# A hybrid of convolution attention, additive attention and a mixture of experts on one core: another ordering rule for TensorE's work in the planner

## What is computed

```python
# layer 0, x is group-normed, (4, 128, 4096)
e1, e2, asm = prelu(w1 @ x), prelu(w2 @ x), prelu(wa @ x)
score = softmax(einsum('nci,ncj->nij', e1, e2), axis=2)
x = x + einsum('nij,ncj->nci', score, asm)
# layer 1, t is the tokens (4, 4096, 128), n = layer norm of t
f, g = n @ W1[:128], n @ W1[128:]
th = tanh(f[:, :, None, :] + g[:, None, :, :] + b1)        # 4096 x 4096 x 16, lower triangle
e = exp(einsum('bija,a->bij', th, w2) + b2) * tril
t = t + einsum('bij,bjh->bih', e / e.sum(-1), n)
# experts: gate, softmax over positions, 8 best positions of each expert, two layers, added back
```

## Time and profile before

| | |
|---|---|
| median of three runs | 6187.79 us |
| the profiled execution, time and span | 6179.02 us, 6177.2 us |
| TensorE busy | 5525.7 us (89%) |
| ScalarE busy | 4999.0 us (81%) |
| VectorE busy, GpSimd busy | 2151.3 us, 2015.0 us |
| mean granted clock of TensorE | 0.947 of full |

### The profile page before, as it was taken

One profiled execution on the slowest core, in us unless ns is written; L12 is line 12 of the kernel. 1 busy time (PEld: TensorE's weight loads), 2 busy tenths in 40 slices (PEclk: granted clock), 3 DMA queues, 4 the chain that ended last, 5 costly groups with the idle time before them and its releaser, 6 DMA issues.

```text
span 6177.2 us, 73459 instructions
## 1 busy us (share of the span) xinstructions
PE 5525.7 (89%) x29478; PEld 1611.1 (26%) x29588; DVE 2151.3 (35%) x3588; ACT 4999.0 (81%) x4234; POOL 2015.0 (33%) x1644
## 2 busy tenths in 40 slices
PE   6999988999999978999999988999999986766756
PEld 2233222222223222222223232222223231111122
DVE  8521137641212257641212257641212161000232
ACT  0127889999888889999888879999888889999930
POOL 0265431124454511124454511125455521111100
PEclk8999999999999989999999979999999998889966
DMA  0000000000000010000000010000000010000037
GB/s 24 1 14 7 8 28 4 1 1 4 11 8 14 8 44 4 1 1 4 11 8 14 9 30 18 1 1 4 8 11 14 8 33 6 1 1 1 11 139 235
DMA packets 31282, 115.99 MB, mean 19 GB/s; under 512 B 4512, under 2 KB 5088, under 8 KB 25632
## 3 DMA queue, kind: packets, MB, share of 16 engines
q1 hardware_dynamic: 30944, 111.30, 5.4%
HBM read 81.60 MB, written 29.49 MB: 18 GB/s over the span
## 4 chain that ended last, share of the span: by engine, by line
PE 69%; issue 13%; ACT 10%; DVE 6%; POOL 2%; DMA 1%; SPq 0%; POOLq 0%; ACTq 0%; DVEq 0%
PE ps L896 24%; PE ps L934 15%; PE ps L920 8%; ACT tanh_slots L836 8%; PE ps L907 6%; PE ps L1012 6%; DVE row_max_parts L1293 3%; PE ps L924 3%; POOL context_and_exp_sums L789 2%; PE ps L974 1%; PE ps L1108 1%; ACT exp_scores L848 1%; PE ps L1053 1%; PE ps L951 1%; DMA eo_scratch<-asm_tokens 1%
## 5 line engine op out<-in xcount | busy, mean ns | idle before, releaser
L836 ACT ACTIVATE tanh_slots<-query_part,key_part 128x2048 f32<-128x2048 f32 (+41 forms) x3072 | 4180.5, 1431 | 233.8 <-PE ps L896 229.3
L896 PE MATMUL ps<-tanh_slots,packed 128*32 128x512 f32 (+2 forms) x18432 | 2324.9, 593 | 356.1 <-ACT tanh_slots L836 328.7
L789 POOL TENSOR_TENSOR context_and_exp_sums<-context_and_exp_sums,exp_scores 128x512 f32<-128x512 f32 (+3 forms) x544 | 648.3, 1196 | 2072.8 <-ACT exp_scores L848 1573.0
L934 PE MATMUL ps<-_tokens_second_and_probs,asm_tokens 128*128 128x512 f32 x2048 | 1015.1, 619 | 1.8 <-DVE tmp_low L1149 1.8
L802 POOL TENSOR_TENSOR conv_prob_sums<-conv_prob_sums,_tokens_second_and_probs 128x512 f32<-128x512 f32 x480 | 612.7, 1276 | 1155.3 <-ACT _tokens_second_and_probs L857 1154.1
L857 ACT ACTIVATE _tokens_second_and_probs<-ps 128x1024 f32<-128x1024 f32 x512 | 519.5, 1015 | 518.5 <-PE ps L924 344.5
L896 PEld LDWEIGHTS ps<-tanh_slots,packed 128*32 128x32 f32 x18432 | 419.3, 112 | 1660.3 <-ACT tanh_slots L836 921.9
L1143 DVE TENSOR_TENSOR context_and_exp_sums<-context_and_exp_sums,ps 128x512 f32<-128x512 f32 (+3 forms) x544 | 345.2, 637 | 1241.1 <-PE ps L907 1239.9
L1293 DVE TENSOR_REDUCE row_max_parts<-ps 128x1 f32<-128x512 f32 x1024 | 653.2, 684 | 300.8 <-PE ps L1012 300.8
L804 POOL TENSOR_TENSOR conv_prob_sums<-conv_prob_sums,_tokens_second_and_probs 128x512 f32<-128x512 f32 x480 | 616.9, 1285 | 37.6
L920 PE MATMUL ps<-e_twice,e_and_minus_max 64*128 64x512 f32 x2048 | 580.4, 644 | 13.7 <-DMA e_and_minus_max<-minus_max_pieces 13.7
(11 more groups left out here) (146 smaller groups left out, 2573.3 us busy)
## 6 DMA issues: line engine op xcount, KB each, us to landing
tanh_slots<-in_wg SPq DMA_DIRECT2D x12, 2048.0 KB, 10.6
y_scratch<-residual_chunks SPq DMA_DIRECT2D x64, 256.0 KB, 2.0
residual_chunks<-y_scratch SPq DMA_DIRECT2D x64, 256.0 KB, 2.8
residual_chunks<-in_x SPq DMA_DIRECT2D x32, 256.0 KB, 2.7
query_part<-in_x SPq DMA_DIRECT2D x4, 1024.0 KB, 5.1
normed_tokens_first<-in_x SPq DMA_DIRECT2D x4, 1024.0 KB, 7.1
p_scratch<-e_twice SPq DMA_DIRECT2D x4, 1024.0 KB, 6.7
query_part<-in_wg SPq DMA_DIRECT2D x2, 2048.0 KB, 13.5
```

The lines of the kernel that those rows point to most:

```text
L789: pool.tensor_tensor(dst, dst, src, ALU.add).then_inc(s_ds, 1)
L836: nc.scalar.activation(S[:, 4 * (R % 2) + k, q:SUP], F[:, SUP * blk.s + q:SUP * blk.s + SUP], ACT.Tanh, bias=keypart(blk.b, kg, kg + 1)).t ...
L896: last = mm(PS[32 * k:32 * k + 32, t, off:CHUNK], w2k[:, g, :], S[:, 4 * (R % 2) + k, CHUNK * t + off:CHUNK * t + CHUNK], start=(g == 0), ...
L934: last = mm(PVB, VT[:, 2 * p + u, :], PROB[:, P % 2, u, :], start=(p == 0 and u == 0), stop=(p == PPC - 1 and u == 1))
```

## The change

It touches the planner alone. No instruction is added or removed; 5324 steps on TensorE are emitted in another order, and so are those of the other engines. In the planner's clock a switch between TR and any other step on TensorE now costs 0.09, and a step that follows another on the same engine is ready at once instead of 0.03 later. The first round of a block is held until VectorE has taken the contexts of all its chunks, not that of its own chunk. The ranks change: C from 1 to 3, QK from 4 to 1, PV from 5 to 1, while TR stays at 2.

```diff
@@ lay_out
-        in_bank = {}
+        in_bank, turned = {}, False
...
+            if e == "PE" and (key[0] == "TR") != turned:
+                turned = not turned
+                span += 0.09
             clock[e] = at + span
...
-                ready[y] = max(ready[y], end + (self.HOP if y[0] != e else 0.03))
+                ready[y] = max(ready[y], end + (self.HOP if y[0] != e else 0.0))
@@ plan
                 behind = [prior_t, prior_tr]
-                if g == 0 and x.before[t] is not None:
-                    behind.append(("DVE", "C", x.before[t], t))
+                if g == 0 and t == x.ts[0]:
+                    behind += [("DVE", "C", x.before[u], u) for u in x.ts if x.before[u] is not None]
                 prior_tr = put("PE", "TR", (R, t), 0.03 + 0.86 * w, behind, 2)
...
-        put("PE", "C", (n, t), 0.05 + 0.86 * w, done, 1)
+        put("PE", "C", (n, t), 0.05 + 0.86 * w, done, 3)
...
-                put("PE", "QK", (P,), 1.25, behind, 4)
+                put("PE", "QK", (P,), 1.25, behind, 1)
...
-                put("PE", "PV", (P,), 1.9, behind, 5)
+                put("PE", "PV", (P,), 1.9, behind, 1)
```

## The result

The change took 6245.63 us (median of 7 runs, 6231.91 to 6262.44) against 6187.79 us of the kernel before (7 runs): ratio 1.0094, 95% interval 1.007 to 1.0117. It is slower by 58 us. The forecast was 6168 us with a range up to 6231 us, and it gave 0.22 to slower.

The account below looks back on a forecast made before the run. TensorE was taken to bound the convolution stages, ScalarE the gate stages and last stretch. 6179 - 65 (stage changes) + 45 (waits) = 6159 us profiled, plus 9 to the median: 6168 us, range 6115 to 6231.

Parts of the forecast that it names:

- The prices of the handovers: On TensorE, each switch costs 0.14 us per run of pieces and 0.20 per run of 128-row steps.
- Rival 5: On TensorE, the handover price stays though pieces are joined, hanging on each PV's entry; near 6270 us; chance 0.05.
- The shift between the stages: Convolution stages get shorter; postponed pieces lengthen maximum stages by 17 us, gate stages by 62, last stretch by 62.
- the sum: Stage-by-stage changes over the kernel: -65 us before waits, most of the convolution stages' 344 us gain given back elsewhere.
- The waits that the new order brings: In the convolution stages, TensorE waits on EX, at 1% in one half and 2.3% in the other: +45 us.
- Rival 3: Convolution stages: slower by TensorE's waits on EX, deciding from 65 us; at 4% the kernel takes 6231 us; chance 0.17.
- Rival 4: Maximum stage: the granted clock falls; at 0.80 the stage takes 365 us, the kernel about 6276; chance 0.06.

Follow-up runs that it names:

- e1_hop_only: Kernel before, with one edit: in the planner a step following another on its own engine is ready at once, on all engines; 6001.9 us, ratio 0.9694.
- e2: Kernel before, with only the change's ranks of QK and PV (1 and 1 instead of 4 and 5); 6250.75 us, ratio 1.0094.
- e3: The change, with the ranks of QK and PV put back to 4 and 5; 6109.1 us, ratio 0.9865.
- e13: The change, with readiness at once on all engines but ScalarE, which stays 0.03 us later; 6170.79 us, ratio 0.9983.
- e6: The change, with readiness at once on TensorE alone, 0.03 us later on the other engines; 6146.12 us, ratio 0.9945.
- e12: The change, with readiness at once on TensorE and ScalarE only, 0.03 us later on the other engines; 6221.64 us, ratio 1.0069.
- e9: Kernel before, with readiness at once on ScalarE alone; pieces on TensorE stay single; 6178.56 us, ratio 0.9984.
- e5: Kernel before, with readiness at once on TensorE alone, 0.03 us later on the other engines; 5992.15 us, ratio 0.9698.

## Why the prediction was wrong

**The prices of the handovers held.** 5.14 us a pair with its two pieces against 5.15, and e1_hop_only, which joins the pieces, is 3% faster. Rival 5 is out.

**The shift between the stages held.** The maximum stage came out to the us, the gate stage and the stretch behind batch 0 within 5. That most of the gain is given back by the ranks was the sum's main point, and e2 and e3 show it by itself: +0.94% on the kernel before, 2.3% on the change.

**The step that failed** is "The waits that the new order brings", +45 us, all of it TensorE's waits on EX in the convolution stages, and nothing in the gate stages and the last stretch. It was short in two places. *Convolution stages:* the four take 587 + 752 + 754 + 749 = 2842 us; the sum had 2717 before waits and 2762 with them. TensorE idles 94 us there instead of some 17 before, and is busy 30 us more than priced. Of the 23 us of its waits in batch 2's stage only 4.3 are on EX; 14 are on VectorE, which the step did not look at. *Last stretch:* 33 us above the sum; exps wait 23 us more than before, tanh tiles 9 more. I gave it 62 us for its moved tiles and no more. In the maximum stage I had worked out that waiting at a block's exps stays inside the slack, and there it does; I didn't repeat that where four pieces take 5.3 us instead of 3.6. In a gate stage ScalarE idles 22 us where e13 has 12, and the stage came out 5 us below the sum even so.

Behind the step stands an edit that I had costed at nothing: readiness at once on the engines other than TensorE. Without it the same change is 92 us faster (e6). That e6's 6146 us lie so near the forecast of 6168 is in part luck: its convolution stages (587, 739, 740 and 739 us) are still 43 us above the sum with its waits, and its three maximum stages 33 below.

**Rival 3 had the sign and not the mechanism.** Waits of PV for EX, its one mechanism, are small. TensorE's waits in batch 2's convolution stage of the change:

```profile
PE ps L937 <- ACT _tokens_second_and_probs L860: 3.8, 10, 0.5
PE ps L910 <- DVE exp_scores L1130: 3.8, 4, 1.3
PE ps L954 <- DVE residual_chunks L1168: 3.1, 1, 3.1
PE ps L937 <- DVE tmp_low L1152: 2.9, 1, 2.9
```

3.8 us in a stage, and 0.5 more in front of QK, is about a third of what was allowed for. The two longest single waits stand at a chunk's boundary, where a PV or a transpose waits for VectorE, and one of them is seen to cost twice:

```profile
3055.82 5.37 PE L937 MATMUL ps<-_tokens_second_and_probs,asm_tokens 128*128 128x512 f32 x8 [2.85 <-DVE tmp_low L1152]
3061.03 0.59 PE L910 MATMUL ps<-exp_scores,_tokens_second_and_probs 128*128 128x256 f32 x2
```

Two PV take 5.21 us behind a wait of 2.85, where a PV costs 1.91 otherwise; the granted clock is 0.62 from 3055.82 to 3058, and 0.98 over the stage. In e6 the stage has its clock at 1.00 and takes 740 us. That isn't owed to its single exps: e12, with rows of exps, takes 741 us at 1.00, and e13, with single ones, 754 at 0.99.

**Rival 4** doesn't show: the clock stayed at 0.99 to 1.00 in the maximum stages.

**Two smaller misses.** I expected TensorE's busy time to fall by some 250 us and it fell by 107; the mean granted clock went from 0.947 to 0.939, and pieces that moved into stages at 0.88 to 0.92 take longer there. That may explain part of it; I didn't split it. And the chances counted a wait only where it would stop TensorE, in a change that rewrites the lists of five engines.

**What stays open.** ScalarE's edit costs about 70 us beside joined pieces (the change against e13, e12 against e6) and nothing alone (e9). Shown is the part of the last stretch, 20 to 30 us that go with the exps' waits. The rest, 10 to 15 us of ScalarE's idle time in a gate stage among it, is located and not explained: the tanh tiles wait for pieces there, and which place in the lists makes them was not tested. In e9 the last stretch does lose 22 us, and the other stages gain as much from a reordering that I did not take apart. Why the convolution stages are 14 us longer where the other engines are ready at once is open too; no kernel changes VectorE's readiness alone. e5's 95 in the last column contain a part of the wait for keys, which priced work doesn't know.

## What to carry to other kernels

When a planner sets the order, count first where each kind of step ends up, stage by stage, and price it by the engine that bounds that stage: a rank that speeds the scarce engine's favourite work can push the rest to where the other engine pays double for it. An edit of the planner's clock acts on the lists of all engines, so read the list of the engine that bounds each stage too, above all for steps in a row that each wait for another engine's next output, and price that output at the clock level it really gets there. And a planner's spans are worth setting to the trace before its ranks are touched: two of them, corrected by 0.09 and 0.13 us, gave 1.4% here.

## What the runs showed of the hardware

A handover between matmuls that use the array in another way has a repeatable price: 0.14 us for a run of 32-column pieces and 0.20 us for a run of 128-row steps, the same in the traces before and after. A further f32 matmul of 512 columns in a run adds 0.86 us, a bf16 one of the maximum stage 0.22.

A short stop of TensorE can cost more than its length. Behind 2.85 us of waiting, two PV took 5.21 us instead of some 3.6. In the last stretch a round of four pieces takes 5.34 us behind a wait of 2.23 and again behind one of 3.93, and 3.64 behind one of 2.58; the slow rounds have the clock at its lower level for most of their length, the fast one has it at the upper throughout.
